# Seven fetched words a block and a float16 difference from the vector engine, in a two-layer graph kernel

## The chip, the cores and the metric

The kernel runs on one core of a Trainium2 chip. The metric is the device time of one execution in microseconds (us), the median of several runs. The engines go by their names in the profile: PE is TensorE, DVE the vector engine, ACT the scalar engine, POOL is GpSimd, SP the queue engine.

## The reference

4096 nodes with 128 features, and a symmetric 0/1 matrix `adj` of 4096 x 4096 with about 17 neighbours a row. Cut to what matters:

```python
h = relu(layernorm(x))
x = x + max_over_neighbours(h, adj)          # layer 0: for each node the feature-wise maximum
h = relu(layernorm(x)) ; wh = h @ W
e = leaky_relu((wh @ a1)[:, None] + (wh @ a2)[None, :])
x = x + elu(softmax(where(adj > 0, e, -9e15), axis=1) @ wh)   # layer 1: attention
```

## The kernel before

The run has three stages.

**Stage A, the maximum over neighbours.** The targets (nodes whose maximum is formed) go in 8 tiles of 512; for each tile the 4096 possible neighbours go in 16 steps of 2 x 128. That makes 128 steps, numbered g (tile q = g // 16, place p = g % 16). In a step PE turns a piece of `adj` (`flip`, eight products of 128x128), counts within each 128 neighbours (`rank`), picks the values of the first neighbour by a one-hot matrix `first` (`pick`, four products of 512 columns), and forms "words" (`digest`, 16 products of 128x128 a step, and in even steps one of 512 columns). `edge_t` is the turned 0/1 matrix, `first` the selector of each first edge, both float16. A word stands for a small group of neighbours that are left when the first is taken away, and is the row number of that group's maximum in the table `subset_max` in DRAM. The word is a sum over edges with weights `bit_w`, minus the sum over first selectors with weights `bit_n` (= -`bit_w`). ACT writes `edge_t` (L441), `first` (L448) and the word keys (L454). DVE takes the maximum of what was picked (`take`, L901 and L904), and keeps the best eight words of each step (L914). Behind each tile it sorts the words of four blocks of 128 targets (`rank_words`, p = 3 to 6, L928 to L934). POOL then fetches 8 rows a block from `subset_max` with indirect DMAs (L412), one instruction a word, and DVE reduces the 8 rows in three halvings (`halve`, L986, L990, L994): blocks 0 and 1 of a tile at p = 15, 0, 1 of a later step, blocks 2 and 3 at p = 8, 9, 10. `found` is a ring of NG = 4 blocks, and DVE executes in order, so a halving that waits for a fetch holds `take` too, and PE's `pick` waits for `take` two steps back (there are two `pick_ps`).

**The spills.** A few targets have more than 8 words. For them a list is made for a range of blocks (`SPILLS`): a count by PE (`spill_count`), selector matrices by DVE (L954), a product with the remaining words by PE (`spill_list`, L667, float32), 8 more fetches by POOL (L374), three halvings (`spill_join`), a store to DRAM, a load back and a merge into `left`. The ranges before are 16, 8 and 8 blocks; the first two lie in stage A at g = 74 to 80 and 106 to 110, where PE waits at once for DVE's answer.

**Table of subsets.** At the start DVE forms 11 subset maxima (`chain`, L893, at the steps CHAIN_AT), each saved by POOL (L359) from one of four buffers; the fifth waits until the first buffer's save has landed. POOL's first fetch waits for all saves.

**Stage B and C.** After step 127 the maxima are joined, the second layernorm and the projections follow, and the attention products `mix` start (PE L753, DVE L1171), with the last blocks' fetches, the last spill and the merges put in between by mix number n. From about n = 96 only mixes are left.

What is written by hand sets every order; no planner is in the way. The waits of POOL in stage A pace it by DVE's progress:

```python
for s in range(SLOTS):
    if q < LAST:
        pool.wait_ge(raised, STEPS * (q + 1) + 4 + (r * SLOTS + s) // (2 if q < LAST - 1 else 3))
```

Of the kernel before, what the change touches and what calls it, by code (L numbers as in the profile page):

```python
# [8 lines left out]
P = 128  # L9
N = 4096  # L10
D = 128
# [23 lines left out]
RANKS = 16  # L35
EPS = 1e-5
# [7 lines left out]
def gnn_two_layers(nc, x, adj, w, a, out):  # L44
    ctx = ExitStack()
    with ctx:
# [18 lines left out]
        with ExitStack() as maxima:  # L65
            best = sb("best", [P, N], F32, maxima)
            left = sb("left", [P, C, D], F32, maxima)
            found = sb("found", [P, NG, SLOTS, D], F32, maxima)
# [16 lines left out]
def layers(nc, adj, x_rows, w, a, edge_units, subset_max, spill_max, out_rows, w_sb, a12, w_in, hs, x1_in, h_hi, h_lo, ident_h, ident32, order_w, bit_w, bit_n, word,  # L85
# [4 lines left out]
    with ctx:  # L90
# [7 lines left out]
        FIRSTS = 6  # L98
        KEYED = 8
# [7 lines left out]
        first = sb("first", [P, FIRSTS, W], F16)  # L107
        limit = sb("limit", [P, 4, TI], F32)
# [13 lines left out]
        spill_rows = sb("spill_rows", [P, 3, SLOTS + 1], I32)  # L122
        spill_to = sb("spill_to", [P, 3], F32)
# [31 lines left out]
        first_ready = sem("first_ready")  # L155
# [3 lines left out]
        gathered = [[sem(f"gathered{i}_{k}") for k in range(4)] for i in range(NG)]  # L159
# [13 lines left out]
        CHAIN_AT = (0, 1, 2, 3, 6, 8, 10, 12, 14, 16, 18)  # L173
# [32 lines left out]
        SPILLS = ((0, 16), (16, 24), (24, 32))  # L206
# [3 lines left out]
        spill_perm = [r.rearrange("p (c d) -> p c d", d=P) for r in (spare_room[:, 0:2048], spare_room[:, 3072:4096], spare_room[:, 0:1024])]  # L210
        spill_found = [r.rearrange("p (s d) -> p s d", d=D) for r in (spare_room[:, 2048:3072], spare_room[:, 2048:3072], spare_room[:, 1024:2048])]
        spill_left = [r.rearrange("p (c d) -> p c d", d=D) for r in (spare_room[:, 0:2048], spare_room[:, 3072:4096], spare_room[:, 0:1024])]
        spill_ps = lambda k: key_ps if k < 2 else banks[5]
        spill_of = lambda g: 0 if g < 4 else 1 if g < 6 else g - 4
# [60 lines left out]
        with nc.Block() as block:  # L275
# [66 lines left out]
            def _(pool):  # L342
# [26 lines left out]
                def spill_fetch(k):  # L369
                    pool.wait_ge(spill_listed, k + 1)  # L370
                    if k == 1:
                        pool.wait_ge(spill_out, 16)
                    for s in range(SLOTS):
                        nc.gpsimd.indirect_dma_start(spill_found[k][:, s, :], None, subset_max,  # L374
                                                     bass.IndirectOffsetOnAxis(spill_rows[:, k, s:s + 1], 0)).then_inc(spill_in, 16)

                def spill_store(k):
                    if k == 0:
# [3 lines left out]
                                                 spill_found[k][:, 0, :], None).then_inc(spill_out, 16)  # L382

                def spill_load(k):
                    lo, hi = SPILLS[k]
                    pool.wait_ge(spill_out, 16 * (k + 1))
                    nc.gpsimd.dma_start(spill_left[k][:, 0:hi - lo, :], spill_dram[:, lo:hi, :]).then_inc(spill_back, 16)

                for n in range(C):
                    q, r = n // ROWS, n % ROWS  # L390
                    if n in (4, 6, 8, 10):
                        i = n // 2 - 2
# [3 lines left out]
                    if n in (20, 28):  # L396
                        spill_store((20, 28).index(n))
                    if n in (21, 28):
                        spill_load((21, 28).index(n))
                    if n == 31:  # L400
                        spill_store(2)
                        spill_load(2)
# [3 lines left out]
                    for s in range(SLOTS):  # L406
                        if q < LAST:
                            pool.wait_ge(raised, STEPS * (q + 1) + 4 + (r * SLOTS + s) // (2 if q < LAST - 1 else 3))
                        elif n > LAST * ROWS or s >= 3:
                            b, t = (n, s - 3) if s >= 3 else (n - 1, SLOTS + s - 3)  # L410
                            pool.wait_ge(gathered[b % NG][t % 4], 32 * (b // NG) + 16 * (t // 4 + 1))
                        nc.gpsimd.indirect_dma_start(found[:, n % NG, s, :], None, subset_max,  # L412
                                                     bass.IndirectOffsetOnAxis(rows_at[:, n, s:s + 1], 0)).then_inc(gathered[n % NG][s % 4], 16)
# [185 lines left out]
            def _(pe):  # L599
# [814 lines left out]
```

## Time and profile before

| | us |
|---|---|
| median of 3 runs (lowest, highest) | 709.78 (709.57, 710.31) |
| the profiled execution | 712.34 |
| its span | 710.5 |
| PE busy | 640.5 (90%) |
| DVE busy | 566.0 (80%) |
| POOL busy | 368.9 (52%) |

Busy times are shares of the whole span; the stages differ, so they are read stage by stage. Idle time on an engine that nobody waits for costs nothing.

### The profile page before, as it was taken

The numbers are of one execution on the slowest core, as the hardware profiler recorded it, in microseconds if no ns is written. First come the engines' busy times: TensorE is split into PE (matmuls) and PEld (weight loads), VectorE is DVE, ScalarE is ACT, GpSimd is POOL, SyncE is SP. The second block draws the span as 40 slices with busy tenths as digits, with TensorE's granted clock in tenths as the row PEclk, the third lists the DMA queues.
The fourth block names the chain that finished last, engine by engine and source line by source line (L and its number), as shares of the span: only waits on it lengthen the run. The fifth ranks groups of instructions, "written<-read, shape, count | busy, mean of one in ns | idle before, by whom it ended". The sixth has DMA issues, their size and how long they took to land.

```text
span 710.5 us, 15875 instructions
## 1 busy us (share of the span) xinstructions
PE 640.5 (90%) x6200; PEld 527.0 (74%) x6200; DVE 566.0 (80%) x1296; ACT 301.5 (42%) x555; POOL 368.9 (52%) x357
## 2 busy tenths in 40 slices
PE   1797999999999999999899678898769999999994
PEld 1465777677777676777667468798669999999994
DVE  8847885887968767779598896995877999989893
ACT  2763666666666646666466536041132210101000
POOL 1430137777777765777777775565300754304030
PEclk9998999999999989999999989899799999999998
DMA  8999999999999996999985935275214444344300
GB/s 269 326 358 384 386 396 346 341 393 394 393 372 346 347 315 214 331 239 390 386 293 188 258 85 181 91 123 201 96 60 160 152 149 173 140 149 178 119 17 18
DMA packets 66925, 173.32 MB, mean 244 GB/s; under 512 B 7984, under 2 KB 12720, under 8 KB 62624
## 3 DMA queue, kind: packets, MB, share of 16 engines
q1 hardware_dynamic: 53776, 138.75, 55.0%
q0 software_dynamic: 13072, 33.51, 16.1%
q8 instruction: 52, 0.85, 0.5%
q14 instruction: 25, 0.20, 0.1%
HBM read 125.37 MB, written 46.86 MB: 242 GB/s over the span
## 4 chain that ended last, share of the span: by engine, by line
PE 67%; DVE 16%; DMA 7%; POOL 4%; issue 4%; ACT 1%; SPq 0%; DVEq 0%; POOLq 0%
PE pick_ps L753 22%; PE pick_ps L635 13%; PE late_ps L651 7%; PE late_ps L650 7%; PE late_ps L611 6%; PE order_ps L620 6%; DVE first L1171 5%; DMA found<-subset_max,rows_at 3%; DMA subset_max<-keys 2%; PE late_ps L646 2%; DVE acc L904 1%; POOL found L412 1%; POOL h_lo L353 1%; DVE x L1029 1%; POOL keys L374 1%
## 5 line engine op out<-in xcount | busy, mean ns | idle before, releaser
L412 POOL DMA_INDIRECT found<-subset_max,rows_at x256 | 260.7, 1018 | 102.5 <-issue 68.2
L753 PE MATMUL pick_ps<-keys,first 128*128 128x129 f32 x1792 | 217.8, 283 | 21.5 <-DVE first L1171 21.5
L753 PEld LDWEIGHTS pick_ps<-keys,first 128*128 128x128 f32 x1792 | 213.2, 199 | 26.8 <-DVE first L1171 25.0
L1171 DVE SCALAR_TENSOR_TENSOR first<-limit,curves_sb,stage 128x512 f32<-128x512 f32 x256 | 200.5, 821 | 17.4 <-PE pick_ps L753 3.4
L904 DVE TENSOR_TENSOR acc<-pick_ps,acc 128x1024 f32<-128x1024 f32 x120 | 146.7, 1223 | 66.1 <-PE pick_ps L635 64.0
L448 ACT ACTIVATE first<-order_ps 128x1024 f16<-128x1024 f32 x128 | 131.1, 1024 | 139.8 <-PE order_ps L620 139.8
L651 PE MATMUL late_ps<-bit_n,first 128*128 128x128 f16 x1024 | 130.3, 221 | 0.0
L650 PE MATMUL late_ps<-bit_w,edge_t 128*128 128x128 f16 x1024 | 130.2, 221 | 0.0
L651 PEld LDWEIGHTS late_ps<-bit_n,first 128*128 128x128 f16 x1024 | 101.3, 99 | 8.0 <-issue 0.3
L611 PEld LDWEIGHTS late_ps<-ident_h,stage 128*128 128x128 f16 x1024 | 69.3, 100 | 46.8 <-DMA stage<-adj 9.8
L635 PE MATMUL pick_ps<-first,h_hi 128*128 128x512 f16 x256 | 98.9, 386 | 5.4 <-DVE acc L904 4.9
L650 PEld LDWEIGHTS late_ps<-bit_w,edge_t 128*128 128x128 f16 x1024 | 101.2, 99 | 0.4
L635 PE MATMUL pick_ps<-first,h_lo 128*128 128x512 f16 x256 | 98.7, 385 | 0.0
L611 PE MATMUL late_ps<-ident_h,stage 128*128 128x128 f16 x1024 | 80.3, 223 | 14.2 <-DMA stage<-adj 9.5
L620 PE MATMUL order_ps<-edge_t,order_w 128*128 128x512 f16 x256 | 77.9, 386 | 0.3 <-ACT first L448 0.3
L441 ACT ACTIVATE edge_t<-late_ps 128x512 int32<-128x512 int32 x128 | 75.7, 591 | 4.4 <-PE late_ps L611 4.4
L420 POOL TENSOR_SCALAR keys<-keys 128x512 f32<-128x512 f32 x7 | 12.8, 1834 | 117.9 <-ACT keys L542 117.8
L914 DVE MAX8 best_words<-keys 128x8 f32<-128x128 f32 x256 | 61.0, 280 | 0.1
L542 ACT ACTIVATE keys<-pick_ps,acc 128x128 f32<-128x128 f32 x28 | 8.0, 367 | 97.8 <-DVE acc L1182 97.8
L620 PEld LDWEIGHTS order_ps<-edge_t,order_w 128*128 128x128 f16 x256 | 25.3, 100 | 31.1 <-issue 2.3
L635 PEld LDWEIGHTS pick_ps<-first,h_hi 128*128 128x128 f16 x256 | 25.5, 99 | 21.5 <-issue 7.0
L454 ACT ACTIVATE keys<-late_ps 128x512 f32<-128x512 f32 x64 | 38.5, 602 | 3.8 <-PE late_ps L651 3.8
(189 smaller groups left out, 552.7 us busy)
## 6 DMA issues: line engine op xcount, KB each, us to landing
stage<-adj SPq DMA_DIRECT2D x64, 1024.0 KB, 11.0
edge_units<-edge_t SPq DMA_DIRECT2D x64, 512.0 KB, 11.0
stage<-edge_units SPq DMA_DIRECT2D x32, 1024.0 KB, 4.8
subset_max<-keys POOLq DMA_DIRECT2D x13, 512.0 KB, 8.5
found<-subset_max,rows_at POOLq DMA_INDIRECT x256, 6.6
best<-x SPq DMA_DIRECT2D x4, 512.0 KB, 6.5
subset_max<-x POOLq DMA_DIRECT2D x4, 512.0 KB, 10.8
spill_max<-keys POOLq DMA_DIRECT2D x4, 512.0 KB, 7.6
```

The source lines that it names most:

```text
L412: nc.gpsimd.indirect_dma_start(found[:, n % NG, s, :], None, subset_max, bass.IndirectOffsetOnAxis(rows_at[:, n, s:s + 1], 0)).then_inc(ga ...
L441: nc.scalar.activation(edge_t[:, g % (KEPT * KEEP), :].bitcast(I32), flip_i[:, :], ACT.Copy, scale=ONE_BITS).then_inc(edge_ready, 1)
L448: nc.scalar.activation(first[:, g % FIRSTS, :], order_ps[:, :], ACT.Relu, scale=-1.0, bias=1.0 - MARK).then_inc(first_ready, 1)
L611: last = nc.tensor.transpose(flip_ps[:, c * TI + r * P:c * TI + (r + 1) * P], low[:, (s * PAIR + c) * P:(s * PAIR + c + 1) * P], ident_h[: ...
L620: last = nc.tensor.matmul(order_ps[:, c * TI:(c + 1) * TI], order_w[:, :], edge_t[:, g % (KEPT * KEEP), c * TI:(c + 1) * TI], start=True, ...
L635: last = nc.tensor.matmul(pick_ps[g % 2][:, c * TI:(c + 1) * TI], half_h[:, p * PAIR + c, :], first[:, g % FIRSTS, c * TI:(c + 1) * TI], s ...
L650: nc.tensor.matmul(key_ps[:, r * P:(r + 1) * P], edge_t[:, g % (KEPT * KEEP), at:at + P], bit_w[:, b, :], start=False, stop=False)
L651: last = nc.tensor.matmul(key_ps[:, r * P:(r + 1) * P], first[:, g % FIRSTS, at:at + P], bit_n[:, b, :], start=False, stop=r == ROWS - 1 a ...
L753: last = nc.tensor.matmul(out_ps(q, b), weight[:, n % WEIGHTS, b * P:(b + 1) * P], wh[:, c, :], start=c == 0 and starts(q, b), stop=c == C ...
L904: V.tensor_tensor(acc[:, q % 2, :], pick_ps[g % 2][:, :], acc[:, q % 2, :], ALU.max).then_inc(raised, 1)
L914: V.max(best_words[:, q % 2, r, g * SLOTS:(g + 1) * SLOTS], key_ring[:, n % KEYED, r * P:(r + 1) * P]).then_inc(maxed, 1)
L1171: V.scalar_tensor_tensor(out=weight[:, n % WEIGHTS, :], in0=limit[:, q % 4, :], scalar=slope[:, c:c + 1], in1=units[:, m % EDGES, k * TI:( ...
```

## The change

1. `digest`: in odd steps of a pair the two products by `edge_t` x `bit_w` and `first` x `bit_n` become one, `rest` x `bit_w`, with `rest = edge_t - first` written by DVE (`rests`, 128x1024 float16, one for two steps, 64 in all).
2. Seven words a block are fetched (FETCHES) instead of eight; the list of the spills takes the words from the eighth on, so more targets spill.
3. Four spill ranges of 8 blocks instead of three; the first three in stage A at COUNT_AT = 42, 74, 106 and LIST_AT = 46, 78, 110, on `order_ps`, with PE waiting for the answers only after the next `pick`. The list's product is float16, in two parts (a word and what rounding left of it, `spill_split`).
4. Chains 4 to 10 stand two steps later; the clearing of `spill_max` two blocks earlier.

```diff
-        CHAIN_AT = (0, 1, 2, 3, 6, 8, 10, 12, 14, 16, 18)
+        COUNT_AT, LIST_AT = (42, 74, 106), (46, 78, 110)
+        CHAIN_AT = (0, 1, 2, 3, 8, 10, 12, 14, 16, 18, 20)
...
-        SPILLS = ((0, 16), (16, 24), (24, 32))
+        SPILLS = ((0, 8), (8, 16), (16, 24), (24, 32))
...
-                    if n in (18, 26, 30):
-                        spill_fetch((18, 26, 30).index(n))
+                    if n in (10, 18, 26, 30):
+                        spill_fetch((10, 18, 26, 30).index(n))
...
-                    for s in range(SLOTS):
+                    for s in range(FETCHES):
                         if q < LAST:
-                            pool.wait_ge(raised, STEPS * (q + 1) + 4 + (r * SLOTS + s) // (2 if q < LAST - 1 else 3))
+                            pool.wait_ge(raised, STEPS * (q + 1) + 4 + (r * FETCHES + s) // (2 if q < LAST - 1 else 3))
...
-                        pe.wait_ge(first_ready, 2 * n + 2)
+                        pe.wait_ge(first_ready, 2 * n + 1)
+                        pe.wait_ge(rest_ready, n + 1)
...
+                            if g % 2:
+                                last = nc.tensor.matmul(key_ps[:, r * P:(r + 1) * P], rest[:, n % RESTS, at:at + P], bit_w[:, b, :],
+                                                        start=False, stop=r == ROWS - 1 and b == QUAD - 1)
+                            else:
...
+                def rests(n):
+                    g = 2 * n + 1
+                    dve.wait_ge(first_ready, g + 1)
+                    if n >= RESTS:
+                        dve.wait_ge(digested, 2 * (n - RESTS + 1))
+                    V.tensor_tensor(rest[:, n % RESTS, :], edge_t[:, g % (KEPT * KEEP), :], first[:, g % FIRSTS, :], ALU.subtract).then_inc(rest_ready, 1)
...
+                rests(0)
                 for g in range(PAIRS):
                     q, p = g // STEPS, g % STEPS
                     take(g)
+                    if g % 2 and g + 2 < PAIRS:
+                        rests(g // 2 + 1)
...
-                        V.tensor_tensor(found[:, at, 0:4, :], found[:, at, 0:4, :], found[:, at, 4:8, :], ALU.max).then_inc(halved, 1)
+                        V.tensor_tensor(found[:, at, 0:3, :], found[:, at, 0:3, :], found[:, at, 4:7, :], ALU.max).then_inc(halved, 1)
```

On PE, in stage A, half a `digest` before (an even step; the pair of products L650 and L651 stands eight times behind the one by `word`):

```order
L611 MATMUL late_ps<-ident_h,stage 128x128 x8
L646 MATMUL late_ps<-word,ones_h 128x512
L650 MATMUL late_ps<-bit_w,edge_t 128x128
L651 MATMUL late_ps<-bit_n,first 128x128
L650 MATMUL late_ps<-bit_w,edge_t 128x128
```

and now, at the same place:

```order
L618 MATMUL late_ps<-ident_h,stage 128x128 x8
L654 MATMUL late_ps<-word,ones_h 128x512
L662 MATMUL late_ps<-bit_w,edge_t 128x128
L663 MATMUL late_ps<-bit_n,first 128x128
L662 MATMUL late_ps<-bit_w,edge_t 128x128
L663 MATMUL late_ps<-bit_n,first 128x128
L659 MATMUL late_ps<-bit_w,rest 128x128 x2
```

Of every eight products six are left, so 12 a step instead of 16.

On DVE, at p = 4 and 5 of a tile (the sorting of words), before:

```order
L904 TENSOR_TENSOR acc<-pick_ps,acc 128x1024
L914 MAX best_words<-keys 128x8 x2
L929 MAX tops<-best_words 128x8
L930 SCALAR_TENSOR_TENSOR vacant<-tops,vacant 128x8
L931 SCALAR_TENSOR_TENSOR rows_at<-tops,vacant 128x8
L933 MATCH_REPLACE best_words<-tops,best_words 128x64
L934 MAX tops<-best_words 128x8
```

and now, at p = 5:

```order
L918 TENSOR_TENSOR acc<-pick_ps,acc 128x1024
L925 TENSOR_TENSOR rest<-edge_t,first 128x1024
L935 MAX best_words<-keys 128x8 x2
L950 MAX tops<-best_words 128x8
L951 SCALAR_TENSOR_TENSOR vacant<-tops,vacant 128x8
L952 SCALAR_TENSOR_TENSOR rows_at<-tops,vacant 128x8
L954 MATCH_REPLACE best_words<-tops,best_words 128x64
L955 MAX tops<-best_words 128x8
```

The subtraction stands behind every second `take`, ahead of the maxima and the sorting; PE's next `digest` waits for it.

On POOL, from block 4 to the middle of stage B, the indirect fetches (`found`), those of the spills (`keys<-subset_max`), stores (`spill_max<-keys,spill_rows`) and loads, before:

```order
28 L412 DMA found<-subset_max,rows_at 128x128 x16
29 L381 DMA spill_max<-keys,spill_rows 4224x128
30 L412 DMA found<-subset_max,rows_at 128x128 x8
31 L387 DMA keys<-spill_max 128x2048
32 L412 DMA found<-subset_max,rows_at 128x128 x40
33 L374 DMA keys<-subset_max,spill_rows 128x128 x8
34 L412 DMA found<-subset_max,rows_at 128x128 x16
```

and now:

```order
27 L384 DMA keys<-subset_max,spill_rows 128x128 x8
28 L419 DMA found<-subset_max,rows_at 128x128 x21
29 L391 DMA spill_max<-keys,spill_rows 4224x128
30 L419 DMA found<-subset_max,rows_at 128x128 x7
31 L397 DMA keys<-spill_max 128x1024
32 L419 DMA found<-subset_max,rows_at 128x128 x28
33 L384 DMA keys<-subset_max,spill_rows 128x128 x8
34 L419 DMA found<-subset_max,rows_at 128x128 x21
```

The fetches of a block are 7 instead of 8, and spill work (8 fetches, a store, a load) comes once for every 8 blocks.

## Rows read from the trace of the kernel before

**Rows 1.** The page's head, and the chain that ended last, by engine.

```profile
span 710.5 us, 15875 instructions
...
PE 67%; DVE 16%; DMA 7%; POOL 4%; issue 4%; ACT 1%; SPq 0%; DVEq 0%; POOLq 0%
```

**Rows 2.** Stretches: length, busy us (count) of PE, PEld, DVE, ACT, POOL, PE clock, DMA share, GB/s.

```profile
180.00:210.00 30.00, 30.00 (x337) 21.65 (x335) 22.76 (x56) 19.52 (x32) 23.23 (x25) 1.00 1.04 380
...
600.00:630.00 30.00, 30.00 (x266) 29.52 (x265) 26.85 (x39) 2.46 (x6) 7.89 (x5) 1.00 0.42 150
```

**Rows 3.** Timeline, PE in steps of stage A: start, duration, line.

```profile
280.69 0.38 PE L635 MATMUL pick_ps<-first,h_hi 128*128 128x512 f16 x1
...
282.43 0.38 PE L646 MATMUL late_ps<-word,ones_h 128*128 128x512 f16 x1
...
282.64 0.22 PE L650 MATMUL late_ps<-bit_w,edge_t 128*128 128x128 f16 x1
...
283.54 0.38 PE L635 MATMUL pick_ps<-first,h_hi 128*128 128x512 f16 x1
```

**Rows 4.** Timeline, DVE in the same steps and behind them, [idle before <- releaser].

```profile
279.37 1.22 DVE L904 TENSOR_TENSOR acc<-pick_ps,acc 128x1024 f32<-128x1024 f32 x1
280.51 0.48 DVE L914 MAX8 best_words<-keys 128x8 f32<-128x128 f32 x2
...
282.01 1.22 DVE L904 TENSOR_TENSOR acc<-pick_ps,acc 128x1024 f32<-128x1024 f32 x1
...
298.21 1.23 DVE L904 TENSOR_TENSOR acc<-pick_ps,acc 128x1024 f32<-128x1024 f32 x1 [1.02 <-PE pick_ps L635]
```

**Rows 5.** Groups of DVE with two inputs in SBUF, 90 to 390 us: count, busy, mean ns.

```profile
L986 DVE TENSOR_TENSOR found<-found 128x1024 f32<-128x1024 f32 x12 | 14.6, 1213 | 5.5 <-DMA found<-subset_max,rows_at 5.5
L990 DVE TENSOR_TENSOR found<-found 128x512 f32<-128x512 f32 x12 | 8.1, 673 | 0.0
```

**Rows 6.** Timeline, a DVE row and the POOL row that starts under it.

```profile
129.19 0.68 DVE L908 TENSOR_TENSOR best<-acc 128x512 f32<-128x512 f32 x1
...
129.27 1.43 POOL L412 DMA_INDIRECT found<-subset_max,rows_at  x1 [0.30 <-issue]
```

**Rows 7.** Timeline, POOL: the first fetch of all, the 16th, and the first of block 24.

```profile
101.14 1.06 POOL L412 DMA_INDIRECT found<-subset_max,rows_at  x1 [9.34 <-DVE acc L904]
...
120.02 0.94 POOL L412 DMA_INDIRECT found<-subset_max,rows_at  x1 [0.30 <-issue]
...
369.18 0.94 POOL L412 DMA_INDIRECT found<-subset_max,rows_at  x1 [0.30 <-DVE acc L904]
```

**Rows 8.** Timeline: first halving, that at g = 120, chain 4, PE's last step of stage A.

```profile
126.92 1.23 DVE L986 TENSOR_TENSOR found<-found 128x1024 f32<-128x1024 f32 x1 [3.61 <-DMA found<-subset_max,rows_at]
...
382.78 1.21 DVE L986 TENSOR_TENSOR found<-found 128x1024 f32<-128x1024 f32 x1
...
54.64 1.22 DVE L893 TENSOR_TENSOR keys<-x 128x1024 f32<-128x1024 f32 x1 [8.22 <-DMA subset_max<-keys]
...
399.58 0.22 PE L651 MATMUL late_ps<-bit_n,first 128*128 128x128 f16 x1
```

**Rows 9.** The chain that ended last, PE around the first spill list: start, length, what.

```profile
257.17 0.86 PE pick_ps L635 x4
258.92 4.56 PE late_ps L667 x32
266.36 1.71 PE pick_ps L635 x4
269.88 0.86 PE pick_ps L635 x4
```

**Rows 10.** Waits of PE, 50 to 400 us: us in total, times, longest.

```profile
PE late_ps L646 <- DVE spill_at L943: 2.6, 2, 1.7
```

**Rows 11.** Timeline, stage B: DVE's longest wait for a spill load.

```profile
498.67 0.69 DVE L976 TENSOR_TENSOR left<-left,keys 128x512 f32<-128x512 f32 x1 [8.48 <-DMA keys<-spill_max]
```

**Rows 12.** DMA issues, 120 to 180 us: count, size, median us to landing.

```profile
stage<-adj SPq DMA_DIRECT2D x11, 1024.0 KB, 15.1
```

More of the change, by code:

```diff
@@ L35 @@
 RANKS = 16
+FETCHES = 7
+LIST = RANKS + 1 - FETCHES
 EPS = 1e-5
@@ L98, in layers @@
         FIRSTS = 6
+        RESTS = 3
         KEYED = 8
@@ L107, in layers @@
         first = sb("first", [P, FIRSTS, W], F16)
+        rest = sb("rest", [P, RESTS, W], F16)
         limit = sb("limit", [P, 4, TI], F32)
@@ L209, in layers @@
         weight = first.rearrange("p s w -> p (s w)").bitcast(F32).rearrange("p (s t) -> p s t", t=TI)
[L210 to L214, printed above, removed]
+        spill_room = [spare_room[:, i * 1024:(i + 1) * 1024] for i in range(4)]
+        spill_perm = [spill_room[i][:, 0:512].bitcast(F16).rearrange("p (c d) -> p c d", d=P) for i in range(2)]
+        spill_left = [spill_room[i].rearrange("p (c d) -> p c d", d=D) for i in range(2)]
+        spill_found = [spill_room[2 + i].rearrange("p (s d) -> p s d", d=D) for i in range(2)]
+        spill_ps = lambda k: order_ps[:, 0:TI] if k < 3 else banks[5]
+        spill_of = lambda g: g // 2 if g < LAST else 4
         spill_dram = spill_max[0:N, :].rearrange("(p c) d -> p c d", c=C)
@@ L666, in spill_list @@
                     for n in range(lo, hi):
-                        last = nc.tensor.matmul(spill_ps(k)[:, 0:SLOTS + 1], spill_perm[k][:, n - lo, :], tops[:, n, SLOTS:RANKS + 1],
-                                                start=n == lo, stop=n == hi - 1)
+                        for part in range(2):
+                            last = nc.tensor.matmul(spill_ps(k)[:, 0:LIST], spill_perm[k % 2][:, n - lo, :], spill_words[:, part, n - lo, :],
+                                                    start=n == lo and part == 0, stop=n == hi - 1 and part == 1)
                     last.then_inc(spill_put, 1)
@@ L944, in spill_slots, with spill_split @@
                                            op0=ALU.add, op1=ALU.mult).then_inc(spill_seen, 1)
+                def spill_split(k):
+                    lo, hi = SPILLS[k]
+                    words = tops[:, lo:hi, FETCHES:RANKS + 1]
+                    if k:
+                        dve.wait_ge(spill_put, k)
+                    sort_step(V.tensor_copy(spill_words[:, 0, :, :], words))
+                    V.tensor_tensor(spill_words[:, 1, :, :], words, spill_words[:, 0, :, :], ALU.subtract)
                 def spill_cuts(k, lo, hi):
-                    first_block, end = SPILLS[k]
+                    start, end = SPILLS[k]
                     dve.wait_ge(spill_seen, k + 1)
-                    if k == 0 and lo == first_block:
+                    if k == 0 and lo == start:
                         for i in range(4):
                             dve.wait_ge(saved[i], 64 if i == 3 else 48)
-                        dve.wait_ge(spill_clear, 64)
                     for n in range(lo, hi):
-                        last = V.tensor_scalar(spill_perm[k][:, n - first_block, :], places[:, :], spill_at[:, n:n + 1], None, ALU.is_equal)
+                        last = V.tensor_scalar(spill_perm[k % 2][:, n - start, :], places[:, :], spill_at[:, n:n + 1], None, ALU.is_equal)
                     if hi == end:
@@ L975, in spill_merge @@
                     dve.wait_ge(reduced, hi)
-                    V.tensor_tensor(left[:, lo:hi, :], left[:, lo:hi, :], spill_left[k][:, lo - at:hi - at, :], ALU.max).then_inc(spill_done, 1)
+                    V.tensor_tensor(left[:, lo:hi, :], left[:, lo:hi, :], spill_left[k % 2][:, lo - at:hi - at, :], ALU.max).then_inc(spill_done, 1)
                 halves = [0]
```

138 lines of the change are left out of this document (73 added, 65 removed).

## The prediction, made before the run

> **What bounds the kernel now.** I read the chain that ended last first: 67% of it is PE [rows 1]. The stretches say where: in stage A (to 399.6 us, the last product of step 127 [rows 8]) PE is busy for all 30.00 us of a stretch at clock 1.00, DVE for 22.76 and POOL for 23.23; in stage C PE is full again, with only mixes [rows 2]. The change leaves stage C alone, so it is worth what it does to stage A and to the waits of stage B.
>
> A step of stage A by PE's rows: an even step runs from the pick at 280.69 to the pick at 283.54, 2.85 us, of which the 16 word products take from 282.64 to 283.54, 0.90 us or 0.056 each [rows 3]. The odd step lacks the product by `word` (282.43 to 282.64, 0.21 us), so it is 2.63; two steps are 5.48 us and a tile of 16 is 43.9.
>
> DVE follows with slack in most steps (it waits 1.02 us for the pick), but where words are sorted (p = 3 to 6 of each tile) one step of DVE is as long as PE's: from `take` to `take` 2.64 us, without a wait between [rows 4].
>
> POOL is the hidden one. A busy share of 23.23 in 30 [rows 2] looks like slack, but its rows have 0.30 us of issue between them: 16 fetches run from 101.14 to 120.02, one each 1.25 us [rows 7], 40 us a tile of 43.9. From its first fetch to the first of block 24 (200 fetches, 8 of them for a spill) 268.0 us go by [rows 7]; some 8 of these it sat paced by DVE, which leaves 1.30 us a fetch, with the stores, loads and held fetches in it. DVE meets POOL at the halvings: the first waited 3.61 us for fetches whose last was issued at 120.02 and that ended at 126.9, so 6.8 us lie between issue and data [rows 7, 8].
>
> **The change, part by part.**
>
> *Word products.* Four of 16 a step go: 4 x 0.056 = 0.22 us a step [rows 3], so two steps take 5.04 instead of 5.48 and a tile 40.3 instead of 43.9. Over 128 steps 28 us, if PE stays the bound.
>
> *The subtraction.* 64 on DVE. No row shows a float16 operation with two SBUF inputs. The nearest are the halvings, float32: 1213 ns for 1024 elements, 673 ns for 512 [rows 5]. They bound it: 1.21 us at one element a cycle, 0.67 if two float16 go together; nothing excludes either by the rows. I take 0.67, of which some 0.60 counts on DVE, since an instruction starts before the one ahead is reported done (`take` is 1.22 long and the next row starts 1.14 behind [rows 4]). The choice rests on both inputs and the output being dense float16, not on a row.
>
> The Trainium skill (VectorE: DVE Perf Modes, the tier table) says the same of a `tensor_tensor` with all operands 16 bit in SBUF: two elements a cycle; its formula with half the elements gives (512 + 151) / 0.96 = 691 ns, as an estimate. No run here has shown it yet.
>
> Is there room? DVE works 22.76 / 30 of 43.9 = 33.3 us a tile [rows 2]. Eight subtractions add 4.8, the shorter first halvings (three slots instead of four, a quarter of 1.21 us, twice) give back 0.6: 37.5 against PE's 40.3. On the average yes, not where words are sorted. There four steps of 2.64, one reduction of about 0.44 and two subtractions are 12.2 us against 10.1 of PE. Carried step by step, `take` is 2.1 us late at p = 7, and the subtraction behind it ends 1.8 us after its start. PE's digest stands 1.74 us behind its pick (280.69 to 282.43 [rows 3]) and now waits for that subtraction; from one odd pick to that digest are 2.41 + 1.74 = 4.15, a free DVE would be done at 1.03 + 1.8 = 2.85, so 1.3 us of lateness are free and 0.85 us a tile become a new stall of PE. Seven tiles have it: 6 us.
>
> *Fetches.* POOL issues 28 instead of 32 a tile, 35 us of 40.3. But spills now come earlier and more often: ahead of block 24 they are 16 fetches, two stores and two loads instead of 8, one and one. So 168 + 16 = 184 fetches instead of 200, 184 x 1.30 = 239 us, and 4.6 for a further store and load.
>
> And the subtraction holds POOL. The DVE row of 0.68 us at 129.19 has two SBUF inputs; the fetch that starts under it, at 129.27, takes 1.43 instead of 0.94 [rows 6]. A fetch starting anywhere else under such a row keeps 0.94 in this trace. About half of the subtractions (0.67 of 1.25 us) will meet a start and hold it 0.33 on the average: 0.17 each, some 50 up to g = 120, so 8.5 us.
>
> The Trainium skill (SBUF — State Buffer, practical consequences) has it that a `tensor_tensor` with both inputs in SBUF contends with GpSimd's reads but does not delay descriptor generation, which it calls inferred; the row at 129.27 speaks against that last part. By the page the 8.5 us would be nothing.
>
> *The start.* Chain 4 waited 8.22 us for a save, until 54.64 [rows 8]. Two steps later it waits less, 5 us gained at that place; but the last save also moves two steps, and POOL's first fetch waits for all of them. I get that fetch at 100.3 instead of 101.14. The 14 fetches of blocks 0 and 1 are issued by 100.3 + 13 x 1.25 = 116.6 and there at 123.4; PE and DVE would be at that halving at 115. So the first tile and a half gain 3.5 us (126.9 to 123.4 [rows 8]), not ten.
>
> *Spill lists.* Before, PE stood for DVE's answers. The first list: picks start at 257.17, 266.36 and 269.88 [rows 9], 12.7 us for two steps of 5.5, so 7.2 lost, with 4.56 of float32 products and a pick at half clock (1.71 for 0.86). The second list has half the products, 3.5. Counts: 2.6 us of waiting [rows 10] and their products. 14 us in all. Now eight small count products (0.5) and 16 float16 products (16 x 0.06 = 1.0) a range, with the answers behind the next pick: 1.5 to 1.6, three times, 4.8 us. DVE's added splits, joins and merges fall partly into sorting steps, 3 us. Gain 6.
>
> **The sum.** Two chains lead to the halving at g = 120 (382.78 before [rows 8]).
> - PE and DVE: 124.4 (the first halving and a cold pick) + 88 x 2.52 = 221.8, + 0.85 x 6, + 4.8, + 3 = 359.1.
> - POOL: 100.3 + 239 + 4.6 + 8.5 + 6.8 = 359.2.
>
> They tie, and with two ties each takes turns in waiting; I add 4 us for this and for the clock: 363. Behind it 399.6 - 382.8 = 16.8 us were left [rows 8], less 7 x 0.22: stage A ends at 378, 21 us earlier. Stage B: up to the last spill's fetches nothing waited for POOL; then DVE waited 8.48 us for the load back, until 498.67 [rows 11], behind eight spill fetches and block 30's eight; with seven 1.25 us less, and short halvings, 0.3. Stage C as before. 21 + 1.6 = 22.6. The profiled execution of 712.34 us has a span of 710.5 [rows 1], and stands 2.6 above the median of 709.78; from the median: **687 us**.
>
> **The rivals.**
> 1. *The tie goes to POOL more clearly.* If POOL is held longer (0.35 instead of 0.17 us a subtraction, or its wait for a spill store is on its way each time, 3 us), g = 120 comes at 370 to 376 and the time is 694 to 700. For it: POOL has no slack left; against: seven fetches for eight. Chance 0.22.
> 2. *The subtraction runs at one element a cycle* (1.21 us, the upper row [rows 5]). DVE has 33.3 + 8 x 1.13 - 0.6 = 41.7 us a tile, the stall behind sorting grows to some 2.5, and nine in ten subtractions hold a fetch by half their length, 0.5 each, 25 us in all: POOL's chain ends at 376, stage A at 391, 700 to 705 us. Chance 0.09.
> 3. *DMA becomes the bound.* The loads of `adj` take 15.1 us to land between 120 and 180 us [rows 12]; they are issued seven steps ahead, 19.2 us before, 17.7 now, and the DMA share there is 1.04 [rows 2]. If faster steps let them queue past 17.7, PE waits in `flip` and gains nothing from 120 to 220 us: 9 us lost, but POOL goes on meanwhile, so 4 to 6 remain: 692. Chance 0.12.
> 4. *Slower: the fetches starve.* If each subtraction holds POOL by e, its chain reaches g = 120 at 350.7 + 50 e; it undoes the gain of all other parts when this passes 382.8 + 3, so from e = 0.7 us on. That takes subtractions of 1.21 us that hold whole fetches, wherever they meet: at e = 1, 725 us. The rows at 129 show a hold only at a start, which speaks against. Chance 0.06.
> 5. *The change helps more*: no tie, PE at the halvings on time, lateness of DVE hidden: 678 to 683. Chance 0.11.
>
> My forecast has 0.40. **Range** 678 to 702: it takes in rivals 1, 3, 5 and the better half of 2. A change within 0.2% (1.4 us) is about what cannot be told from none. Faster 0.91, within 0.03, slower 0.06.
>
> **What would show it.** Subtractions near 0.67 us; two steps in 5.04 us between picks in light stretches; a wait of PE's digest for `rest` of about 0.9 us once a tile at p = 8; fetches of more than 1.2 us under subtractions; the first halving still waiting, some 8 us, to about 123; waits at the halvings of g = 96 to 120; stage A over at about 378; the last wait for the spill load some 1.3 us shorter relative to the end of stage A. It is wrong if the subtraction is twice as long, if POOL is far behind or ahead of PE at g = 120, or if `flip` waits for loads.

## The result and the profile after

| | before | after |
|---|---|---|
| median (lowest, highest), us | 709.67 (709.43, 710.31) | 687.75 (685.59, 688.2) |
| ratio, 95% interval | | 0.9684 (0.9662 to 0.9705) |
| the profiled execution, us | 712.34 | 688.20 |

The change makes the kernel 3.2% faster, 22 us. The page's head and the chain that ended last (beside [rows 1]):

```profile
span 686.4 us, 14958 instructions
...
PE 49%; DVE 22%; issue 10%; POOL 9%; DMA 7%; ACT 2%; SPq 0%; DVEq 0%; POOLq 0%
```

The stretches, columns as in [rows 2]:

```profile
120.00:128.00 8.00, 3.13 (x12) 1.49 (x13) 5.36 (x9) 0.60 (x3) 6.17 (x7) 0.58 1.03 328
180.00:210.00 30.00, 29.31 (x306) 20.15 (x304) 27.49 (x61) 20.38 (x35) 22.97 (x22) 1.00 1.02 332
600.00:630.00 30.00, 30.00 (x265) 29.52 (x265) 26.85 (x40) 2.46 (x6) 8.10 (x6) 1.00 0.47 161
```

Stage C is what it was. In stage A PE is no longer full (29.31 of 30) and DVE nearly is: 27.49, where it was 22.76 [rows 2]. PE's share of the chain fell from 67% [rows 1] to 49%, DVE's rose from 16 to 22.

The timeline of DVE: two steps between `take`s in a stretch without sorting, then the halvings that answer to [rows 8], the last but one in stage A with its wait, and the wait for the last spill load, [rows 11]:

```profile
102.60 1.23 DVE L918 TENSOR_TENSOR acc<-pick_ps,acc 128x1024 f32<-128x1024 f32 x1 [1.01 <-PE pick_ps L642]
105.01 1.23 DVE L918 TENSOR_TENSOR acc<-pick_ps,acc 128x1024 f32<-128x1024 f32 x1 [0.19 <-PE pick_ps L642]
107.64 1.22 DVE L918 TENSOR_TENSOR acc<-pick_ps,acc 128x1024 f32<-128x1024 f32 x1 [1.01 <-PE pick_ps L642]
...
122.64 0.96 DVE L1014 TENSOR_TENSOR found<-found 128x768 f32<-128x768 f32 x1 [7.74 <-DMA found<-subset_max,rows_at]
...
337.59 0.96 DVE L1014 TENSOR_TENSOR found<-found 128x768 f32<-128x768 f32 x1 [0.65 <-DMA found<-subset_max,rows_at]
...
362.17 0.94 DVE L1014 TENSOR_TENSOR found<-found 128x768 f32<-128x768 f32 x1
...
473.39 0.69 DVE L1004 TENSOR_TENSOR left<-left,keys 128x512 f32<-128x512 f32 x1 [8.61 <-DMA keys<-spill_max]
```

107.64 - 102.60 is 5.04 us, as worked out. From the first halving to that at g = 120 (the row at 362.17) go 239.5 us, where it was 255.9 [rows 8].

What PE waited for from 50 to 385 us (total, times, longest), beside [rows 10]; `issue` stands for a wait to which the profile gives no releaser:

```profile
PE late_ps L654 <- ACT first L455: 10.8, 12, 1.5
PE pick_ps L642 <- DVE acc L915: 5.6, 1, 5.6
...
PE late_ps L654 <- issue: 2.6, 1, 2.6
PE order_ps L627 <- DVE spill_at L964: 2.3, 3, 0.8
```

L654 is the start of `digest`. It waits for two things, `first` by ACT and `rest` by DVE, and the profile names the first; the timeline says which it is. DVE's `take` at p = 5 of a tile and the subtractions behind those of p = 5 and 7, then PE's `digest` in this tile and the next:

```profile
222.03 1.23 DVE L918 TENSOR_TENSOR acc<-pick_ps,acc 128x1024 f32<-128x1024 f32 x1
223.17 0.68 DVE L925 TENSOR_TENSOR rest<-edge_t,first 128x1024 f16<-128x1024 f16 x1
...
229.07 0.68 DVE L925 TENSOR_TENSOR rest<-edge_t,first 128x1024 f16<-128x1024 f16 x1
```

```profile
223.96 0.38 PE L654 MATMUL late_ps<-word,ones_h 128*128 128x512 f16 x1 [1.30 <-ACT first L455]
...
229.85 0.38 PE L654 MATMUL late_ps<-word,ones_h 128*128 128x512 f16 x1 [0.69 <-ACT first L455]
...
267.56 0.38 PE L654 MATMUL late_ps<-word,ones_h 128*128 128x512 f16 x1 [0.71 <-ACT first L455]
```

The subtractions end at 223.85 and 229.75, and `digest` starts 0.1 us behind each, at 223.96 and 229.85. It can't be `first` that held it: the subtraction needs a later `first` itself before it can start. All thirteen waits of L654 in the table end 0.1 us behind a subtraction, the one put down to issue too. Ten of them lie between the first halving and g = 120, 8.6 us together: one at p = 8 in each of six tiles, 0.69 each, where 0.85 was foreseen, and one at p = 6 in each of the last four, 0.71 to 1.30, which was not.

### The profile page after: what moved, and what is told of

It is laid out like the page before. It is cut to its first block, busy times and chain, and to the rows that moved or that the text cites. A ratio compares the mean times of both kernels' runs of the same rounds, so it can differ in the third digit from the quotient of the medians.

```text
span 686.4 us, 14958 instructions
## 1 busy us (share of the span) xinstructions
PE 603.2 (88%) x5688; PEld 488.4 (71%) x5688; DVE 600.3 (87%) x1377; ACT 301.4 (44%) x555; POOL 355.1 (52%) x335
## 4 chain that ended last, share of the span: by engine, by line
PE 49%; DVE 22%; issue 10%; POOL 9%; DMA 7%; ACT 2%; SPq 0%; DVEq 0%; POOLq 0%
PE pick_ps L765 20%; PE pick_ps L642 9%; POOL found L419 6%; DMA found<-subset_max,rows_at 5%; PE order_ps L627 5%; DVE first L1207 5%; DVE acc L918 5%; PE late_ps L618 5%; PE late_ps L663 2%; PE late_ps L659 2%; PE late_ps L662 2%; POOL keys L384 2%; DVE best_words L935 2%; PE late_ps L654 1%; DVE x L1057 1%
## 5 line engine op out<-in xcount | busy, mean ns | idle before, releaser
L419 POOL DMA_INDIRECT found<-subset_max,rows_at x224 | 235.9, 1053 | 88.8 <-issue 58.7
L765 PEld LDWEIGHTS pick_ps<-keys,first 128*128 128x128 f32 x1792 | 210.9, 197 | 27.7 <-DVE first L1207 26.2
L663 PE MATMUL late_ps<-bit_n,first 128*128 128x128 f16 x512 | 84.7, 219 | 0.0
L662 PE MATMUL late_ps<-bit_w,edge_t 128*128 128x128 f16 x512 | 84.7, 219 | 0.0
L659 PE MATMUL late_ps<-bit_w,rest 128*128 128x128 f16 x512 | 70.5, 219 | 0.0
L663 PEld LDWEIGHTS late_ps<-bit_n,first 128*128 128x128 f16 x512 | 50.0, 98 | 7.8
L662 PEld LDWEIGHTS late_ps<-bit_w,edge_t 128*128 128x128 f16 x512 | 50.0, 98 | 0.2
L925 DVE TENSOR_TENSOR rest<-edge_t,first 128x1024 f16<-128x1024 f16 x64 | 44.4, 694 | 0.0
```

The costliest lines, as they stand in the source:

```text
L659: last = nc.tensor.matmul(key_ps[:, r * P:(r + 1) * P], rest[:, n % RESTS, at:at + P], bit_w[:, b, :], start=False, stop=r == ROWS - 1 and ...
L662: nc.tensor.matmul(key_ps[:, r * P:(r + 1) * P], edge_t[:, g % (KEPT * KEEP), at:at + P], bit_w[:, b, :], start=False, stop=False)
L663: nc.tensor.matmul(key_ps[:, r * P:(r + 1) * P], first[:, g % FIRSTS, at:at + P], bit_n[:, b, :], start=False, stop=False)
L765: last = nc.tensor.matmul(out_ps(q, b), weight[:, n % WEIGHTS, b * P:(b + 1) * P], wh[:, c, :], start=c == 0 and starts(q, b), stop=c == C ...
```

## The experiments

Each is timed against the kernel before on the same chip. The ratios are to that kernel; the changed kernel's is 0.9684. The chips differ a little (medians of the kernel before from 709.67 to 710.9 us), so a small difference between two variants is read from the ratios, or from rows of their traces.

**First, undo parts.** The edits, on the kernel before (e1) and on the changed one (e2 to e4):

```diff
e1, before + rest/products only
+                            if g % 2: rest x bit_w
+                            else: edge_t x bit_w, first x bit_n
e2, changed, old products and no subtraction
-                    if g % 2 and g + 2 < PAIRS:
-                        rests(g // 2 + 1)
e3, changed, eight words (and two buffers for `rest` instead of three, for which DVE never waits)
-FETCHES = 7
+FETCHES = 8
e4, changed, a slower operation for the same difference
-                    V.tensor_tensor(rest, edge_t, first, ALU.subtract)
+                    V.scalar_tensor_tensor(out=rest, in0=edge_t, scalar=1.0, in1=first, op0=ALU.mult, op1=ALU.subtract)
```

> The kernel before with the word products of the change alone: rest = edge_t - first by the vector engine (two buffers), six products for eight; eight words a block, spills and chains as before (the fetches' arrivals are counted on three semaphores instead of four). Theory (two chains): POOL now bounds, 200 fetches x 1.30 us + 50 holds x 0.17 bring the halving at g = 120 to about 376 us (382.8 before), so 703 to 705 us. Rival (PE alone bounds stage A): 88 x 0.22 us less the stall behind the sorting, 368, so 695.

> The changed kernel with the eight products of before and no subtraction; seven words, four lists and the chains as changed. Theory: PE's chain rules with 2.74 us a step and no stall behind the sorting: first halving at 122 to 123, g = 120 at about 371, 697 us. Rival (POOL alone bounds the changed kernel): POOL has the same fetches without the holds, so no slower than 688, perhaps 680.

> The changed kernel with eight words fetched a block (two rest buffers instead of three for room). Theory (two chains): POOL needs 208 fetches x 1.30 + 4.6 + 8.5 us and reaches g = 120 at about 390 instead of 362, the time is 708 to 716. Rival (PE alone bounds): only the first halving comes 2.5 us later and the halvings are longer, 690 to 692.

> The changed kernel with the subtraction as a scalar_tensor_tensor (times 1.0, then subtract), which is expected to run at one element a cycle, 1.21 us instead of 0.69. Theory: DVE has 41.7 us a tile, the stall behind the sorting grows to some 2.5 us and more fetches are held: 698 to 705 us. Rival (DVE has room, PE's step bounds): under 2 us, 688 to 690. If the instruction also takes 0.69 us, the time is unchanged and nothing is told.

| | median (range), us | ratio (95%) |
|---|---|---|
| e1 products and subtraction alone | 714.42 (712.39 to 719.87) | 1.0068 (1.0039 to 1.0097) |
| e2 all but these | 691.63 (689.78 to 696.7) | 0.9751 (0.9696 to 0.9807) |
| e3 eight words | 719.45 (718.1 to 719.88) | 1.0119 (1.0082 to 1.0156) |
| e4 subtraction of 1217 ns | 707.76 (704.02 to 710.18) | 0.9956 (0.9933 to 0.9979) |

All four fell outside what I expected. The products that take 28 us of PE away are worth 4 to 5 us beside the other parts. The medians give 3.9 us (691.63 to 687.75) and the ratios 4.8, but the intervals of the two ratios overlap a little; the traces are clearer, where stage A ends at 381.62 in e2 and at 376.25 in the changed kernel. By themselves the products gain nothing: e1 is 0.7% slower. Seven words instead of eight are worth some 31 us beside them (30.9 by the ratios), and the sum of both changes is far from the sum of each. No run has the seven words, the four lists or the later chains alone, so e2's 18 us are not shared out among these. Why eight words don't go with the products stands in DVE's waits, 50 to 405 us of e3 and 50 to 400 us of e1:

```profile
DVE found L1014 <- DMA found<-subset_max,rows_at: 27.8, 7, 9.9
...
DVE keys L996 <- DMA keys<-subset_max,spill_rows: 8.1, 2, 5.3
```

```profile
DVE found L1000 <- DMA found<-subset_max,rows_at: 13.5, 4, 5.1
```

36 us of waiting for fetches in e3, against 8.4 in the changed kernel, 7.7 of it at the first halving; in e1 13.5, where it was 5.5 before. With 32 fetches a tile POOL is the bound in e3, and whatever PE gains ends at a halving. In e1 PE also waits 6.4 us for the answer to a spill's count (2.6 before [rows 10]), and its stage A ends only 0.9 us earlier, at 398.64 [rows 8].

e4 puts 0.54 us on each subtraction. Between the first halving and g = 120 there are 44, which makes 24 us more for DVE, and 16 of them arrive (255.9 us from the one to the other, where the changed kernel takes 239.5); the whole run is 20 us longer. DVE has little slack left. e4 also gives the hold of POOL a second point. Groups of POOL's fetches (count, busy, mean ns), 125 to 360 us, of e2 (no subtraction), the changed kernel and e4:

```profile
L419 POOL DMA_INDIRECT found<-subset_max,rows_at x155 | 154.2, 995 | 56.0 <-issue 43.9 <-DVE rows_at L948 9.7 <-DVE acc L914 1.8
```

```profile
L419 POOL DMA_INDIRECT found<-subset_max,rows_at x155 | 161.7, 1043 | 48.0 <-issue 39.6 <-DVE acc L918 6.9 <-DVE rows_at L952 0.9
```

```profile
L419 POOL DMA_INDIRECT found<-subset_max,rows_at x144 | 160.3, 1113 | 49.0 <-issue 36.6 <-DVE acc L918 6.8 <-DVE rows_at L953 5.4
```

(1043 - 995) x 155 = 7.4 us for the 44 subtractions of this stretch, 0.17 each, as put. Counted fetch by fetch, 26 of the 44 have a fetch that starts under them, and these 26 take 8.0 us more than 0.94 each. With subtractions of 1217 ns a fetch is 118 ns longer than in e2.

It is not only a fetch at the start of such a row that is held, as the prediction says. In the kernel before, this one starts 0.59 us behind the start of the first halving (126.92, 1.23 long [rows 8]), and all eleven fetches that start under L986 there between 100 and 360 us take 1.25 to 1.99 us:

```profile
127.51 1.45 POOL L412 DMA_INDIRECT found<-subset_max,rows_at  x1 [0.30 <-issue]
```

The halving goes on for another 0.64 us, and the fetch is 0.51 longer than 0.94. The held fetches under L986 all follow this: what is left of the DVE operation at their start, less some 0.12 us.

**Second, is it an order that can be mended?** Beside the other parts, products and subtraction gave 4 to 5 us of PE's 28. Either the place of the subtraction is at fault, or DVE's amount of work.

```diff
e5, changed
-                    take(g)
                     if g % 2 and g + 2 < PAIRS:
                         rests(g // 2 + 1)
+                    take(g)
e6, changed
-        CHAIN_AT = (0, 1, 2, 3, 8, 10, 12, 14, 16, 18, 20)
+        CHAIN_AT = (0, 1, 2, 3, 8, 9, 10, 12, 13, 14, 16)
e7, changed: PE waits behind the count and the list at once
-                    if g - 1 in COUNT_AT:
-                        pe.wait_ge(spill_seen, COUNT_AT.index(g - 1) + 1)
+                        pe.wait_ge(spill_seen, COUNT_AT.index(g) + 1)
e8, changed: e5 + e6, and words sorted at these places
-                    if q >= 1 and 3 <= p < 7:
+                    if q >= 1 and p in (3, 4, 6, 8):
```

> The changed kernel (687.75 us) with the subtraction of an odd step put ahead of the `take` of that step on DVE. Theory: what is left of PE's waits in stage A is the digest's wait for `rest` (some 13 us, which the trace puts down to ACT's `first`, L654, and to issue), because the digest bears only 1.3 us of DVE's lateness while the pick, which waits for the `take` of two steps back, bears some 3. With the subtraction 1.2 us earlier the lateness is borne: the waits of L654 fall to under 4 us, stage A ends 6 to 9 us earlier, 679 to 681. Rival: DVE's amount of work bounds, so that the wait moves from digest to pick (L642) one for one: 687 to 688. Rival 2: POOL is right behind PE; then the halvings at g = 96 to 120 wait for fetches, 685.

> The changed kernel (687.75 us) with chains 5 to 10 at the steps 9, 10, 12, 13, 14, 16 instead of 10, 12, 14, 16, 18, 20, so the last save is written four steps earlier. Theory: the wait of 7.7 us at the first halving (122.6) is for fetches that start at 99.6, and these wait for the last save; with it four steps of 2.5 us earlier the first fetch is at 88 to 92, the halving waits at most 1 us and stage A ends 4 to 6 us earlier: 682 to 684. Rival: the denser chains (1.2 us each on DVE) and their stores hold DVE and PE by what is gained (fifth buffer's saves are waited for again, as 8.2 us in rows 8), or POOL's pace after the start bounds: 686 to 689.

> The changed kernel (687.75 us) with PE waiting for DVE's answer to a spill's count and list at once, behind the products, instead of behind the next pick. Theory: three counts and three lists then stand open on PE, each for DVE's answer of 0.7 to 1.5 us, six stops, 3 to 7 us in all: 691 to 695; L654's and L627's waits grow by as much. Rival: PE is two picks ahead of DVE there or catches DVE up, so that the stop is given back at the next wait for DVE: 687 to 689.

> The changed kernel with the subtraction ahead of `take`, the early chains, and the sorting of words at the places 3, 4, 6, 8 of a tile instead of 3, 4, 5, 6. Theory: the gains of the first two add (6 to 9 and 4 to 6 us), the spread sorting takes what is left of the lateness (1 to 2): 672 to 678, and waits for fetches at the halvings after the first come up, since POOL has little slack. Rival: POOL is the next bound from the first halving on, so only part of it arrives: 680 to 684, with 5 us or more of waits of L1000 and L1004 for fetches at g = 96 to 120.

| | median (range), us | ratio (95%) |
|---|---|---|
| e5 | 690.74 (685.24 to 691.97) | 0.9686 (0.9638 to 0.9734) |
| e6 | 689.17 (687.95 to 691.6) | 0.9694 (0.966 to 0.9728) |
| e7 | 692.95 (692.02 to 694.46) | 0.9738 (0.9712 to 0.9765) |
| e8 | 688.65 (685.69 to 692.0) | 0.9698 (0.9663 to 0.9733) |

e5 did to the wait just what was meant and nothing to the time. PE's waits for `digest` fell from 13.4 us to 3.7 (with those put down to issue; from 10.8 to 1.2 without), and other waits came up, of PE and of DVE:

```profile
PE pick_ps L642 <- DVE acc L918: 3.6, 2, 3.1
PE order_ps L627 <- DVE spill_at L964: 3.3, 3, 1.5
...
PE late_ps L654 <- ACT first L455: 1.2, 1, 1.2
```

```profile
DVE keys L996 <- DMA keys<-subset_max,spill_rows: 6.3, 2, 3.8
```

So the theory of the place falls. Up to 292 us e5 gains 1.1 us on the changed kernel (145.4 against 146.6 from the halving at 146 to that at 292), and then DVE stands for a spill's fetches: POOL is only a few us behind. e7 hit its range: the waits put back (behind three counts and three lists) cost 5.2 us by the medians, 3.8 by the ratios.

e6 missed its range of 682 to 684. Its first fetch is at 91.12 instead of 99.55, its first halving at 114.89 without a wait, 7.8 us early, and the next halving at 146.19, where the changed kernel has 146.08. PE lost all of it here, and SP's queue shows why:

```profile
135.50 1.03 PE L618 MATMUL late_ps<-ident_h,stage 128*128 128x128 f16 x8 [7.24 <-DMA stage<-adj]
```

```profile
109.36 1.17 SPq L313 DMA_DIRECT2D x<-x  x1
110.99 15.12 SPq L288 DMA_DIRECT2D stage<-adj  x1
126.15 0.80 SPq L295 DMA_DIRECT2D edge_units<-edge_t  x1
```

L313 reads `x` a second time (for stage C), and the load of `adj` issued behind it holds the queue for 15.12 us instead of 0.37. e8 missed both its ranges and has the same stop: its first halving is at 114.31, and PE then stands 4.8 us for a load, until 133.10. The changed kernel has the same rows, under the wait of its first halving:

```profile
107.54 0.87 SPq L313 DMA_DIRECT2D x<-x  x1
110.92 12.74 SPq L288 DMA_DIRECT2D stage<-adj  x1
```

**Third, the amount of work, and the second read of x.**

```diff
e9, changed: the subtraction of 16 columns from the fourth on
+                    to = 2 * TI if n < RESTS else 16
e10, e6 and
-                    if n == UNITS * 4:
+                    if n == LOADS - STAGES:
                         ...
                         sp.dma_start(hs[:, :, :], x_rows)
e11, e8 and the same
e12, changed: one float32 product for the list's two float16
-                        for part in range(2):
-                            last = nc.tensor.matmul(spill_ps(k)[:, 0:LIST], spill_perm[k % 2][:, n - lo, :], spill_words[:, part, n - lo, :],
+                        last = nc.tensor.matmul(spill_ps(k)[:, 0:LIST], spill_perm[k % 2][:, n - lo, :], tops[:, n, FETCHES:RANKS + 1],
```

> The changed kernel with the subtraction cut to 16 of 1024 columns from the fourth one on (so the words of later odd steps are formed from an old difference and the output is another; products, waits and fetches stay as they are). It takes 0.6 us of DVE and the hold of POOL away and leaves the 12 products. Theory (DVE's amount of work bounds the changed kernel from 120 to 376 us, 75.8 busy of 80 in 200 to 280, so that products and subtraction gave only 4 us where the products alone are worth 28): DVE has some 4.7 us less a tile, PE is again busy all the time, a tile takes 40.5 to 41 instead of 42.8, the halving at g = 120 comes at 350 to 354, 674 to 679. Rival: POOL stands right behind (its fetches of a tile take 35 us and the spill work up to 14), then the halvings L1014 wait for fetches by 5 us or more in all after the first one: 680 to 684. Rival 2: the loads of adj are right behind: L618 waits for them 5 us or more: 680 to 684.

> The early chains of e6 (689.17 us), and the second read of x, which the queue of SP issues at 107.5 us (behind it the issue of the next load of adj takes 12.7 to 15.1 us instead of 0.4), put at load 60, some 355 us. Theory: that read made PE wait 7.2 us for a load at 135.5 in e6, and in the changed kernel the same lateness lay under the halving's wait of 7.7; without either the halving of blocks 2 and 3 (146.1 in both) comes at 138 to 140 and all behind it too: 680 to 683. Rival: the loads are late by the DMA engines' load (share 1.04, 400 GB/s until 117) and not by this read, then L618 still waits 5 us or more near 135: 687 to 689. Rival 2: the read costs the same at its new place: 687 to 689, with waits near 360 to 380.

> As e8 (early chains, subtraction ahead of `take`, spread sorting; 688.65 us, its profile 683.8), with the second read of x at load 60. Theory: 6 us below e8's like, 677 to 682, and the best version of all. Rival: DVE's work bounds behind 140 us and the orders on it do nothing, so it equals e10 within 2 us.

> The changed kernel (687.75 us) with the list's product in float32 in one part as before (8 products a range of 10 columns) instead of float16 in two parts. Theory: before, 32 such products took 4.56 us in the chain, so 0.14 each, against 0.06 for one of float16: three lists in stage A of 1.1 us instead of 1.0, and DVE is spared the two splits; with DVE the bound it is no slower: 686 to 689. Rival: float32 products of another engine mode cost PE several times that and PE is the bound: 691 to 694, with the next pick late by 1 us or more at each list.

| | median (range), us | ratio (95%) |
|---|---|---|
| e10 | 680.83 (679.14 to 682.43) | 0.9585 (0.9545 to 0.9625) |
| e11 | 682.98 (678.82 to 685.1) | 0.9633 (0.959 to 0.9676) |
| e12 | 691.35 (688.55 to 693.36) | 0.975 (0.9714 to 0.9787) |

The total of e9 (76,950 us) measures nothing: with other words more targets spilled than the list has room for, and the kernel ran its general path for such inputs behind the fast one. Its stage A is whole, with every product and fetch at its place, so its trace is read there alone. Stretches of 80 us (200 to 280) of e2, the changed kernel and e9:

```profile
200.00:280.00 80.00, 80.00 (x910) 57.80 (x909) 67.55 (x169) 52.20 (x87) 58.58 (x60) 1.00 1.02 342
```

```profile
200.00:280.00 80.00, 75.81 (x809) 52.30 (x807) 75.83 (x186) 53.72 (x90) 62.08 (x60) 1.00 1.02 350
```

```profile
200.00:280.00 80.00, 79.33 (x850) 54.94 (x848) 71.37 (x192) 55.57 (x93) 61.39 (x63) 1.00 1.03 370
```

With the old products PE is full; with the new ones and no subtraction it is nearly full again; with both it idles 4.2 us of 80 and DVE works 95%. The halvings of e9:

```profile
329.05 0.96 DVE L1015 TENSOR_TENSOR found<-found 128x768 f32<-128x768 f32 x1 [0.97 <-DMA found<-subset_max,rows_at]
...
351.57 0.94 DVE L1015 TENSOR_TENSOR found<-found 128x768 f32<-128x768 f32 x1
```

g = 120 comes 10.6 us before the changed kernel's 362.17, and inside the 350 to 354 expected. 0.5 of this is an earlier first halving; the other 10.1 are the price of the subtraction. And the halving before it, at 329.05, waits for its fetches here, 8.5 us before 337.59, where the changed kernel waited for the same fetches: POOL's own chain moved by 8.5 us, 0.5 of them from an earlier first fetch (99.09). Nearly all of the rest is held fetches: the fetches up to there are 7.7 us shorter in sum, and POOL's gaps between them are the same.

e10 hit its range and has the lowest median, 1.0% under the changed kernel (0.9585 / 0.9684). Its queue and its second halving:

```profile
110.63 0.37 SPq L288 DMA_DIRECT2D stage<-adj  x1
...
341.89 0.86 SPq L313 DMA_DIRECT2D x<-x  x1
346.41 12.57 SPq L295 DMA_DIRECT2D edge_units<-edge_t  x3
```

```profile
138.35 0.94 DVE L1014 TENSOR_TENSOR found<-found 128x768 f32<-128x768 f32 x1
```

Where the read now stands only stores of `edge_t` are behind it. The last row is three of them, 4.2 us each, and without a read ahead of them such stores take as long there (in the changed kernel five from 344.13 take 22.96 us), so no cost of the read is seen at its new place. e11 adds the orders of e5 and e8 and is not told from e10. Its halving at 281.35 is 3.5 us ahead of e10's (284.82), and then it waits 3.1 us for a spill's fetches (L996).

e12 is slower by 3.6 us (4.7 by the ratios), the rival's range. The list's products make PE's part:

```profile
L678 PE MATMUL order_ps<-tops,keys 128*128 128x10 f32 x48 | 5.7, 256 | 0.0
```

against 1.6 us for the 48 of float16, so 1.4 us more a list, for which DVE waited too (5.7 us at L987, 1.6 in the changed kernel). From the first halving to g = 120 e12 takes 243.2 us, 3.7 more than the changed kernel.

## Why the prediction was right

687 us were forecast and 687.75 measured, and the steps can be set beside the traces. Of the two chains that should meet at g = 120, POOL's was forecast at 359.2 and comes at some 358.5, as an estimate (its last fetch for that halving is issued at 351.73, and 6.8 us go by to the data). DVE's and PE's was forecast at 359.1 and comes at 362.17. So the mechanism holds, DVE as the second bound included, but that the total is this close is partly luck: a term too small by 3.5 us and 4 us put down for something else cancel.

- **Word products.** Two steps in 5.04 us: as put. From the first halving to that at g = 120 the sum's terms without lateness make 229.6 us (221.8 + 4.8 + 3), and e9, nearly without lateness, takes 229.4. But e2 takes 242.5 with the old products, so they give 13 us there and not 88 x 0.22 = 19. Over half of what is missing (3.6 us) lies between the first two halvings, 21.3 us in e2 and 22.9 in e9, where nine steps should be 2.0 us shorter in e9: PE restarts at a lower clock there in e9 (0.69 on the mean from 120 to 128 us) and not in e2 (1.00). Why the 80 steps behind give 14.7 us and not 17.6 stays open.
- **The subtraction.** 681 ns, 51 times, from 90 to 370 us: the lower bound of [rows 5] was the right choice. By the Trainium skill (VectorE: DVE Perf Modes, the tier table) the estimate was 691 ns, and the trace agrees within 1.5%.
- **The stall behind sorting.** The term that was mis-sized: 0.85 us a tile, 5.1 up to g = 120, where 8.6 were measured. The wait at p = 8 was there, a little shorter than put. The one at p = 6 in four of six tiles was missed, because only p = 7 was carried through step by step. And DVE's load was put too low: 37.5 us a tile. What the change adds was right (4.2 put and measured), but the 33.3 it was added to was scaled from 30 us in a tile without spill work [rows 2]. Over five whole tiles DVE is busy for 181.7 us before (148.48 to 382.78) and 202.6 after (146.08 to 362.17), so 36.3 and 40.5 us a tile.
- **The 4 us for the tie.** They were right in size and wrong in cause. Taking turns cost 0.65 us, the only wait for fetches behind the first halving; PE's wait for `rest` took the place of the rest. 5.1 and 4 make 9.1, and the subtraction's price by e9 is 10.1. That POOL is close behind is shown: its chain just reaches DVE's at 337.59, and versions that make DVE faster wait for fetches soon (e9 at a halving, e5, e8 and e11 for a spill's).
- **Holds.** 0.17 us a subtraction put, 0.17 to 0.18 measured, and 8.5 us of POOL's chain put, 8.1 by e9. The working (half of the subtractions, half of their length) was right; the sentence that a fetch keeps 0.94 anywhere else under such a row was not, and rival 4 leaned on it. The Trainium skill (SBUF — State Buffer, practical consequences) infers that such an operation does not delay descriptor generation; these rows go against it, and the measurement decides.
- **The start.** First fetch 99.55 (100.3 put), first halving 122.64 after a wait of 7.74 (some 8, to 123): as put. PE then restarts at a granted clock of 0.58, and its next step, from the pick at 124.87 to that at 129.05, takes 4.2 us instead of 2.6; one us was put for a cold pick.
- **Spill lists.** Gain 6 put. The two experiments that undo a part of it cost 5.2 (e7) and 3.6 us (e12) by the medians, 3.8 and 4.7 by the ratios, some 8.5 together, before what DVE's added work takes back. What it takes back was not measured by itself.
- **Stage A over** at 376 (last product 376.25) instead of 378; the wait for the last spill load ends 97.1 us later, 99.1 before: 2.0 us, 1.6 put.
- **Rival 3** (loads of `adj`) did not happen, yet it was nearer than put: the lateness was there, from a read of `x` and not from faster steps, under the wait of the first halving. Rival 1 was near too: POOL's chain is 3.6 us ahead at g = 120. Rival 4 needed subtractions that hold more than 0.7 us; e4, with 1.22 us ones, gave 707.76, just under before. e1 and e3, 0.7% and 1.2% over it, show another way to the other side, eight words.

## What to carry to other kernels

Work taken off the bound engine and put on the second one is worth only the gap between the two: here 28 us of PE became 4 to 5, and what paid was that the third engine, POOL, lost an eighth of its fetches for words at the same time (200 fetches ahead of block 24 became 184, since the spills added eight). Take the load of the engine that receives the work over whole periods of the loop, with everything that comes once in several: 30 us of a 44 us tile made DVE's load 33.3 where it was 36.3. A wait hides others that end with it: after taking one away, look at what is late behind it (a queue's issue of 12.7 us was free until the fetches came earlier). The fetches alone gained nothing (e6), with the read moved too it was 7 us (e10); the read moved alone was not run.

## What the runs showed of the hardware

- The second read of `x` (4096 rows of 128 float32, 2 MB) leaves SP's queue in 0.9 to 1.2 us, but the load of `adj` issued next behind it takes 9.03 us in the kernel before, 12.74 in the changed one and 15.12 in e6, against 0.37 in e10, where the read isn't there. This read is paid by what is behind it in its queue; whether by its size or its small rows, no run tells.
- A fetch that starts under a DVE operation with two SBUF inputs (halvings, merges, subtractions) takes longer than 0.94 us by what is left of that operation, less some 0.1 us; a fetch that starts under a `take`, with one input in PSUM, keeps 0.94 (79 of them from 100 to 360 us, none over 0.97). The longest is 1.83 us here and 1.99 in the kernel before. POOL, then DVE under it, in the changed kernel:

```profile
206.42 1.70 POOL L419 DMA_INDIRECT found<-subset_max,rows_at  x1 [0.30 <-issue]
```

```profile
206.36 0.94 DVE L1014 TENSOR_TENSOR found<-found 128x768 f32<-128x768 f32 x1
```

- The same float16 difference of 128x1024 takes 681 ns as a tensor_tensor and 1217 ns as a scalar_tensor_tensor (e4).
- After PE stood still for 5.65 us at the first halving, its granted clock was 0.58 on the mean from 120 to 128 us, so it restarted at about the lower of its two levels, 1.2 GHz (picks of 0.58 to 0.63 us instead of 0.38). In e2, where it stood 3.45 us, the clock stayed at 1.00 from 120 to 200 us.
